# One-core attention and MLP kernel: the first head's roped halves written by the engines, its steps in a new order, and the last pair's tail reordered

## What is computed

```python
qc = layernorm(x @ W_cq)                      # 1024 x 192
q  = qc @ W_q        # 16 heads x (128 "nope" + 64 "pe")
kv = x @ W_ckv       # 16 heads x (64 "pe" + 128 "nope")
kn = layernorm(kv_nope);  k_nope, v = split(kn @ W_kv)
q_pe, k_pe = rope(q_pe), rope(k_pe)
attn_h = softmax(causal(q k^T / sqrt(192))) @ v
# side path: top-8 tokens of each of 8 gates, a small attention over them,
# its mean (one 128-vector for each gate) is added to two heads' output
x1 = layernorm(x + concat(attn_h + io) @ W_o)
up, gate = x1 @ ternary(W_up)^T, x1 @ ternary(W_gate)^T
out = layernorm(x1 + (silu(up) * gate) @ ternary(W_down)^T)
```

## Time and profile before

| what | us |
| --- | --- |
| three runs | 715.3, 719.58, 719.54; median 719.54 |
| profiled execution: its own time | 718.88 |
| profiled execution: span of the core | 717.1 |
| PE busy in the span | 657.5 (92%) |
| DVE, ACT, POOL busy | 468.7, 399.4, 366.4 |

### The profile page before, as it was taken

How to read it: one execution, slowest core, us unless ns; L and a number is a source line. 1 busy time by engine, 2 the same in 40 slices (tenths; PEclk the granted TensorE clock), 3 DMA queues, 4 the chain that set the end, 5 groups by cost and what they waited for, 6 DMA issues and landing times.

```text
span 717.1 us, 14209 instructions
## 1 busy us (share of the span) xinstructions
PE 657.5 (92%) x4502; PEld 594.9 (83%) x4502; DVE 468.7 (65%) x1294; ACT 399.4 (56%) x934; POOL 366.4 (51%) x327
## 2 busy tenths in 40 slices
...
GB/s 244 104 40 210 1 31 89 69 87 53 56 100 88 51 37 117 88 51 18 119 104 51 0 132 110 51 0 117 124 51 0 105 239 67 2 1 1 1 31 30
DMA packets 26895, 51.43 MB, mean 72 GB/s; under 512 B 3824, under 2 KB 17008, under 8 KB 26864
## 3 DMA queue, kind: packets, MB, share of 16 engines
...
...
## 4 chain that ended last, share of the span: by engine, by line
PE 57%; DVE 13%; ACT 10%; issue 10%; POOL 6%; SPq 2%; DMA 2%; DVEq 0%; ACTq 0%; POOLq 0%
PE J L804 9%; PE J L806 9%; PE J L805 9%; PE J L837 4%; DVE PTl L1252 3%; PE SC L824 3%; PE SC L827 3%; PE SC L828 3%; PE SC L826 3%; PE SC L825 3%; POOL rstd L706 3%; ACT kvraw L1207 3%; ACT Pb L1117 3%; ACT PTh L1100 2%; PE J L950 2%
## 5 line engine op out<-in xcount | busy, mean ns | idle before, releaser
L1252 DVE TENSOR_TENSOR PTl<-J,PTh 128x512 fp32r<-128x512 f32 (+1 forms) x192 | 102.2, 553 | 81.8 <-ACT PTh L1100 81.1
L1117 ACT ACTIVATE Pb<-SC,nm 128x128 f32<-128x128 f32 (+7 forms) x128 | 94.7, 740 | 52.2 <-DVE nm L1316 51.4
L1316 DVE CUSTOM_DVE_ANT_0 SC<-SC,mask 128x128 f32<-128x128 f32 (+7 forms) x128 | 97.3, 760 | 34.6 <-PE SC L828 31.2
L1100 ACT ACTIVATE PTh<-J 128x512 fp32r<-128x512 f32 (+1 forms) x192 | 88.1, 491 | 12.7 <-PE J L837 11.8
L804 PE MATMUL J<-PTh,Vh 128*128 128x256 f32 x320 | 88.5, 276 | 4.5 <-DVE PTl L1252 4.4
L837 PE MATMUL J<-ident,Pb 128*128 128x128 f32 x576 | 87.2, 279 | 4.7 <-ACT Pb L1117 4.4
L806 PE MATMUL J<-PTh,Vl 128*128 128x256 f32 x320 | 89.8, 280 | 0.0
L805 PE MATMUL J<-PTl,Vh 128*128 128x256 f32 x320 | 89.7, 280 | 0.0
L824 PE MATMUL SC<-KNh,QNh 128*128 128x128 f32 (+2 forms) x192 | 69.6, 363 | 8.1 <-DMA QS<-RQl 6.1
L837 PEld LDWEIGHTS J<-ident,Pb 128*128 128x128 f32 x576 | 64.2, 142 | 12.0 <-ACT Pb L1117 6.7
L804 PEld LDWEIGHTS J<-PTh,Vh 128*128 128x128 f32 x320 | 60.4, 189 | 9.8 <-DVE PTl L1252 6.7
...
## 6 DMA issues: line engine op xcount, KB each, us to landing
...
```

Of the source, the lines that this page charges most:

```text
L1100: return act.activation(o, i, ACT.Copy)
L1117: act.activation(Pb[i % 2][:, w], SC[i % 2][:, s], ACT.Exp, bias=nm[:, i % 2:i % 2 + 1], scale=-1.0, accum_out=sm[:, b, i:i + 1]).then_inc ...
L1252: dve.tensor_tensor(o, i, h.bitcast(F32), ALU.subtract).then_inc(done[kind], 1)
L1316: dve.tensor_tensor_reduce(out=SC[i % 2][:, s], in0=SC[i % 2][:, s], in1=mask[:, 128 * (7 - i):S], scale=-SCALE, scalar=HIGH, op0=ALU.add, ...
```

## The change

1. **First head's stacks by engines.** ACT and DVE write the two row halves of KD and KL straight from KX (`rk`: two copies and two subtractions of 64x512 in place of one each of 128x512), and DVE writes QS in `rope_q_first`. `stack_k_first` and `stack_q_first` with their twelve DMAs of 128 KB are gone. Head 1 still needs RKh, RKl, RQh and RQl: POOL writes them in new steps `rkrows` and `rqrows`.
2. **Prologue** in a new order: the qc tiles normalized in one operation each (192 columns in place of 128 and 64 twice), `qm` of odd tiles on 64 rows, W_qpe's and W_qps's high parts on ACT (POOL before), the first POOL product of `rkm` as a step `rks` of its own and earlier, `w0p` after the first `qc`, `kv` 1 before `qm`, `qm` 2 and 3 and `wb` last.
3. **Head 0** has a new list (FIRST_HEAD): `side` 0 and 1 in the slot of tile 1, `top8` split from `side` 1 and put in slot 3, `ab`, `qn` of head 1 earlier. SP loads the weights of pair 1 at the end of its prologue, and waits there for the top-8 and `rk_ready` before it loads the side path's weights and W_ip.
4. **Head 1:** `ropek` of pair 1 moves from the end of head 0 to slot 0 of head 1, behind `kvn`; `side` 10 to 12 one slot later; `io` from slot 6 to 4.
5. **All heads:** KD and KL become the two planes of one tile KK, RKh and RKl those of RK, so that `stk` is two DMAs of 512 KB in place of four of 256 KB.
6. **Last pair and MLP:** `wosp`, `rw` and the row additions later, `ln1`, `ln1n` and `ht` 0 one slot earlier, `ug` 0 and 1 in the last slot of head 15; the epilogue's start in a new order; LAG = 7; `res`, `ost`, `onorm` of the third quarter after the last `m`, and the last quarter done tile by tile (`last`, `lnorm`) with two stores.

The diff, cut to its core:

```diff
-LAG = 5
+LAG = 7
...
+        FIRST_HEAD = [
+            ("qk", 0, 0), ("exp", 0, 0), ("qmb", 0, 2), ("qmb", 0, 3),
+            ("qk", 0, 1), ("side", 0, 0), ("side", 0, 1), ("exp", 0, 1), ("kvs", 0, 3), ("kvag", 0, 1), *t(0, 0), ("rk", 0, 1),
+            ("qk", 0, 2), ("exp", 0, 2), ("qp", 0, 1), ("qps", 0, 1), ("ropeq", 0, 1), ("kvn2", 0, 1), *t(0, 1),
+            ("qk", 0, 3), ("qn", 0, 1), ("rqrows", 0, 1), ("kt", 0, 1), ("exp", 0, 3), ("rkrows", 0, 0), ("rkrows", 0, 1),
+            ("ab", 1, 0), ("pv", 0, 0), *t(0, 2), ("top8", 0, 0), ("kvn2", 0, 2), ("vsh", 0, 1), ("wkv", 1, 0),
+            ("qk", 0, 4), ("exp", 0, 4), ("side", 0, 2), *t(0, 3), ("stk", 1, 0), ("stq", 1, 0), ("kvn2", 0, 3), ("vs", 1, 0),
+            ("kt", 1, 0), ("side", 0, 3),
+            ("qk", 0, 5), ("pv", 0, 1), ("exp", 0, 5), ("kt", 1, 1), ("side", 0, 4), ("wosp", 2, 0), ("wqn", 2, 0), ("wqp", 1, 0),
+            *t(0, 4), ("qn", 1, 0), ("wo", 0, 0),
+            ("qk", 0, 6), ("side", 0, 5), ("exp", 0, 6), ("qn", 1, 1), *t(0, 5), ("wo", 0, 1), ("side", 0, 6), ("kv", 1, 0),
+            ("qk", 0, 7), ("kpe", 1, 0), ("side", 0, 7), ("exp", 0, 7), ("kv", 1, 1), ("pv", 0, 2), *t(0, 6),
+            ("side", 0, 8), ("kpe", 1, 1), ("kv", 1, 2), ("kv", 1, 3), ("side", 0, 9)]
...
-                    add(0, True, ("wtot", 0, 2), ("rowadd", 0, 0), ("rowadd", 0, 1))
-                    add(1, True, ("rowadd", 0, 2), ("rowadd", 0, 3), ("tern", 0, 8))
+                    add(0, True, ("wtot", 0, 2))
+                    add(1, True, ("rowadd", 0, 0), ("rowadd", 0, 1), ("rowadd", 0, 2), ("rowadd", 0, 3), ("tern", 0, 8))
                     add(2, True, ("tern", 0, 9))
                     add(3, True, ("tern", 0, 10))
                     add(4, True, ("tern", 0, 11))
-                    add(5, True, ("ln1", 0, 0))
-                    add(6, True, ("ln1n", 0, 0), ("ln1", 0, 1))
-                    add(7, True, ("ht", 0, 0), ("ln1n", 0, 1))
+
+            def late_steps():
+
+                add(4, True, ("ln1", 0, 0))
+                add(5, True, ("ln1n", 0, 0))
+                add(6, True, ("ht", 0, 0), ("ln1", 0, 1))
+                add(7, True, ("ug", 0, 0), ("ug", 0, 1), ("ln1n", 0, 1))
...
+                add(6, last, ("rw", 2, 0))
...
-                add(0, first, ("side", 0, 10))
-                add(1, first, ("side", 0, 11))
-                add(2, first, ("side", 0, 12))
+                add(1, first, ("side", 0, 10))
+                add(2, first, ("side", 0, 11))
+                add(3, first, ("side", 0, 12))
...
                 add(0, more, ("kvn", 1, 0))
+                add(0, first, ("ropek", 1, 0))
                 add(1, more and not first, ("qp", 1, 1), ("ropeq", 1, 0))
                 add(1, more, ("kvn2", 1, 0), ("stk", n, 0))
                 add(2, True, *t(h, 1), ("wo", m, 3))
...
+        PRO_PE = (each("qc", 0, 1, 2, 3) + each("kpe", 0) + each("qc", 4, 5, 6, 7) + each("kv", 0, 1) + each("qm", 0, 1) +
+                  each("ab", 0) + each("kpe", 1) + each("qp", 0) + each("qps", 0) + each("qn", 0) + each("kv", 2, 3) +
+                  each("kt", 0) + each("qm", 2, 3) + each("wb", 0))
+        PRO_ACT = (each("xs", 0, 1, 2, 3) + each("cs", 0) + each("w0", 0) + each("kpe", 0) + each("qnm", 0) + each("kv", 0, 1) +
+                   each("qm", 0, 1) + each("ab", 0) + each("qnm", 1) + each("kpe", 1) + each("rk", 0) + each("qn", 0) +
+                   each("kvn2", 0) + each("kv", 2) + each("kt", 0) + each("kv", 3) + each("qm", 2))
+        PRO_DVE = (each("xs", 0, 1, 2, 3) + each("qc", 0, 1, 2, 3) + each("w0p", 0) + each("w0", 0) + each("qnm", 0) +
+                   each("w0k", 0) + each("qc", 4, 5, 6, 7) + each("kvs", 0) + each("qms", 1) + each("qm", 0, 1) + each("kvs", 1) +
+                   each("kvnh", 0) + each("ab", 0) + each("ropeq", 0) + each("qn", 0) + each("rk", 0) + each("kvs", 2) +
+                   each("kt", 0) + each("qms", 3) + each("wb", 0))
+        PRO_POOL = (each("wkp", 0) + each("wkv", 0) + each("qrs", 0) + each("wqpl", 0) + each("rks", 0) + each("qrs", 1) +
+                    each("rkm", 0) + each("kvnh", 0) + each("rks", 1) + each("rkm", 1) + each("rqrows", 0) + each("vsh", 0) +
+                    each("kvnh", 1) + [("wqn", 1, 0), ("wosp", 1, 0)])
...
-            if q >= 1:
+            if q in (1, 2):
                 a += {1: [one("res", q - 1)], 2: [one("ost", q - 1)], 4: [one("onorm", q - 1)]}.get(e, [])
             return a
 
-        EPILOGUE = [one("ug", 0), one("ug", 1), *t(NH - 1, 7), ("wo", NH - 1, 2), one("ht", 1), ("pv", NH - 1, 3), one("m", 0),
-                    one("ln1", 2), one("ug", 2), one("ug", 3), one("m", 1), ("wo", NH - 1, 3), one("ln1n", 2), one("ug", 4),
-                    one("m", 2), one("ln1", 3), one("ug", 5), one("m", 3), one("dn", 0), one("ug", 6), one("ln1n", 3),
-                    one("m", 4), one("dn", 1)]
+        EPILOGUE = [("wo", NH - 1, 2), *t(NH - 1, 7), one("ug", 2), one("ht", 1), one("m", 0), one("ug", 3), ("pv", NH - 1, 3),
+                    one("m", 1), one("ln1", 2), one("ug", 4), one("m", 2), ("wo", NH - 1, 3), one("ln1n", 2), one("ug", 5),
+                    one("m", 3), one("ln1", 3), one("ug", 6), one("m", 4), one("ln1n", 3)]
         for n in range(7, NM):
             EPILOGUE += mlp_steps_of(n)
-        EPILOGUE += [one("m", NM - 2), one("onorm", 2), one("m", NM - 1)] + [one("dn", n) for n in range(NM - LAG, NM)]
-        EPILOGUE += [one("res", 3), one("ost", 3), one("onorm", 3)]
+        EPILOGUE += [one("m", NM - 2), one("dn", NM - 7), one("m", NM - 1), one("res", 2), one("ost", 2), one("onorm", 2)]
+        EPILOGUE += [one("dn", n) for n in range(NM - 6, NM)] + [one("last", 0), one("last", 1), one("lnorm", 0), one("lnorm", 1)]
...
-                        sp.dma_start(KD[b][rows, :].bitcast(F32), RKh[r, :].bitcast(F32)).then_inc(stacked[b], 16)
-                        sp.dma_start(KL[b][rows, :].bitcast(F32), RKl[r, :].bitcast(F32)).then_inc(stacked[b], 16)
+                        sp.dma_start(KK[b][rows, :, :].bitcast(F32), RK[r, :, :].bitcast(F32)).then_inc(stacked[b], 16)
...
-            stack_q_first(0)
-            stack_k_first(0)
-            stack_k_first(1)
-            stack_q_first(1)
+            load("wkv", 1)
+            load("wqp", 1)
+            sp.wait_ge(side_dve, 2)
+            sp.wait_ge(head1_lo, 1)
+            for n, src in enumerate((W_sq, W_sk, W_sv, W_io[:, 0:128])):
+                sp.dma_start(wside[:, n, :], src).then_inc(ld_ws, 16)
+            sp.wait_ge(rk_ready, 1)
             sp.dma_start(wip, W_ip.rearrange("(k p) n -> p k n", p=128)).then_inc(ld_wip, 16)
...
+            eng.tensor_copy(QS[0][0:64, q], x0[0:64, :]).then_inc(rq0_mul, 1)
             eng.wait_ge(rq0_mul, 2 * c + 2)
-            eng.tensor_tensor(RQl[:, q], X[:, 0, q], RQh[:, q].bitcast(F32), ALU.subtract).then_inc(rq0_ready, 1)
-            if c == 1:
-                eng.wait_ge(rq0_ready, 2)
-                eng.sem_inc(rq_ready, 1)
+            eng.tensor_tensor(QS[0][64:128, q], x0[0:64, :], QS[0][0:64, q].bitcast(F32), ALU.subtract).then_inc(rq0_ready, 1)
...
+                    if kind == "rks":
+                        q = half(c)
+                        gp.wait_ge(k0_swapped[c], 32)
+                        gp.wait_ge(ld_cs[c], 16)
+                        gp.tensor_tensor(KX[:, 1, q], KX[:, 1, q], sinT[:, q], ALU.mult).then_inc(rk0_mul[c], 1)
+                    if kind == "rkrows":
+                        q = half(c)
+                        gp.wait_ge(rk0_mul[c], 3)
+                        gp.tensor_copy(RKh[:, q], KX[:, 0, q]).then_inc(head1_hi, 1)
+                        gp.wait_ge(head1_hi, c + 3)
+                        gp.tensor_tensor(RKl[:, q], KX[:, 0, q], RKh[:, q].bitcast(F32), ALU.subtract).then_inc(head1_lo, 1)
+                        if c == 1:
+                            for n in range(2):
+                                gp.wait_ge(rk0_ready[n], 2)
+                            gp.wait_ge(head1_lo, 4)
+                            gp.sem_inc(rk_ready, 1)
+                    if kind == "rqrows":
+                        q, x0 = half(c), roped_q(c)[0]
+                        gp.wait_ge(rq0_mul, 2 * c + 1)
+                        gp.tensor_copy(RQh[:, q], x0).then_inc(head1_hi, 1)
+                        gp.wait_ge(head1_hi, c + 1)
+                        gp.tensor_tensor(RQl[:, q], x0, RQh[:, q].bitcast(F32), ALU.subtract).then_inc(head1_lo, 1)
+                        if c == 1:
+                            gp.wait_ge(rq0_ready, 2)
+                            gp.wait_ge(head1_lo, 2)
+                            gp.sem_inc(rq_ready, 1)
...
-                    pe.wait_ge(k0_stacked[c], 64)
-                    pe.wait_ge(q0_stacked[c], 32)
+                    pe.wait_ge(rk0_ready[c], 2)
+                    pe.wait_ge(rq0_ready, c + 1)
...
-                        copy(RKh[:, half(c)], KX[:, 0, half(c)]).then_inc(rk0_mul[c], 1)
```

(16 more changed lines are left out.)

186 lines of the change are left out of this document (83 added, 103 removed).

## The result

| | us |
| --- | --- |
| kernel before | median 718.41 of 4 runs (715.3 to 719.58) |
| changed kernel | median 707.86 of 4 runs (707.47 to 708.24) |
| ratio | 0.986, 95% interval 0.9825 to 0.9895 |
| changed kernel, profiled execution | 707.47; span 705.6 |

The change makes the kernel 1.4% faster, 10.6 us by the medians; the forecast was 708. The sum is near, its terms less so. This table takes the start of the first tile of scores of some heads as milestones, in the profiled execution of each kernel (718.88 and 707.47 us, so 11.4 us apart).

The account below looks back on a forecast made before the run. PE bounds the MID passes; elsewhere time goes to DVE's prologue and chains of waits. Head 0 and prologue -12, head 1 +6.8, MID 0, last pair -4.5, end -1.3 sum to -11.0: from 718.88 to 708 us, range 698 to 717.

Parts of the forecast that it names:

- prologue: Up to head 0's first tile: 3.3 us gained, the tile starting at 29.9 us instead of 33.29.
- port: Prologue and head 0: DVE operations using SBUF held up by POOL, 0.1 us for each of ten, 1.0 us in all.
- first tile to head 1: Head 0: 8.7 us gained, with the fifth tile at 44.8 us and head 1 beginning at 87.7 to 88.4.
- head 1: Head 1: 4.2 us lost, as the swap of QX queues behind a stack that waits for the later ropek.
- clock behind it: Start of head 2: PE at the lower clock after its wait, costing 2.6 us.
- loop, the other five pairs: The MID passes: no change, 0 us, with ends of -3 and +3.
- last pair and end: Last pair and MLP: 4.5 us gained in the last pair and 1.3 at the end.
- Rival C: Prologue and head 0: some 17 DVE operations each held 1.0 us by POOL, +15 us, 723 us; chance 0.08.
- top-8 chain: Head 0: from MAX8 to PE's side 2 takes 4.8 us, ending near 51 us.
- rival A: Head 1: the swap doesn't wait behind the stacks, so head 1 gains 3.5 us; 698 us, chance 0.20.
- PE's wait for `ht`: End of head 15: the 2.73 us wait goes, and 1.2 us of lower clock behind it.
- the sign that I had named: End of the kernel: in the trace after, a last dn about 5 us before the span's end.

Follow-up runs that it names:

- experiment 4: Changed kernel with POOL's second half of the first rope waiting for DVE's first KL rows: 706.7 us, ratio 0.9836.
- Experiment 7: Changed kernel with edits of experiment 1 and experiment 4, 15 useless PE matmuls, and POOL's V split waiting for the one-hot: 690.23 us, ratio 0.962.
- 5 to 7: Changed kernel with top-8, side 2 and 3 later: 709.62 us; with experiment 1's and experiment 4's edits: 696.25, plus 18 useless matmuls: 693.96; then Experiment 7.
- experiment 1: Changed kernel with head 2's K stack issued after the swap of QX on SP's queue: 697.0 us, ratio 0.9712.
- 3: Kernel before with only ropek of pair 1 moved to slot 0 of head 1, behind kvn: 725.29 us, ratio 1.0076.
- 9: Two kernels, each the changed kernel with one edit: K stack as four 256 KB DMAs, 708.07 us; LAG back to 5, 707.75 us.
- 8: Kernel before with all last-pair and MLP edits: 712.0 us, ratio 0.9889; with only the moves of weights and row additions: 718.17 us, ratio 0.9986.
- experiment 2: Changed kernel with ropek of pair 1 put back at the end of head 0: 703.69 us, ratio 0.9798.

## Why the prediction was right, and where it wasn't

| step | forecast | changed | what the runs say |
| --- | --- | --- | --- |
| prologue | -3.3 | -1.4 | port, mis-sized |
| first tile to head 1 | -8.7 | -6.7 | port shown by 4 and 7, clock fits 5 to 7; mis-sized |
| head 1 | +4.2 | +2.5 | mechanism shown by 1 and 3 |
| clock behind it | +2.6 | +1.4 | first pair 75.13 us for 73.75; mis-sized |
| loop, the other five pairs | 0 | +0.3 | 9: not the merged stacks |
| last pair and end | -5.8 | -7.6 | 8: -5.6 in its profiled execution, -7.1 by medians |
| sum | -11.0 | -11.5 | |

**Prologue.** What ends PE's waits was forecast rightly in the main; most of what follows is about sizes. The term that was mis-sized here is the port: I took 0.1 us for each of ten DVE operations, and three of them lost 2.3 us (experiment 4). With them free the first tile starts at 30.26; I had said 29.9. The mean of the earlier trace rows, by which I chose 0.1, was of two operations with next to no POOL work beside them; the one held row, i8f in the earlier trace rows, was the one to go by. Rival C had the size right, 0.7 to 1.0 us each, but not the number of operations on the path.

**Head 0.** -12 was forecast by head 1, -8.1 came. 2.0 us were lost by the first tile, and the fifth came at 47.12 for 44.8, 2.3 late. The top-8 chain was 4.5 us, as I said (4.8), but i8f and i8d in it and the one-hot behind it are held for some 2 us together, which I had copied from the old trace as their own durations. Tile 5 came at 58.85 for 55.5. There the clock was at 0.50 over 55 to 60, where I had allowed 0.6 us for it; tile 5 to tile 6 took 10.05 us, not 8.7. Experiment 7 takes both away and reaches head 1 at 85.33.

**Head 1.** The queue and the place of the wait are as forecast, and its length nearly: product 8.92 us behind the rope's end (9.3 forecast), QS landed 4.5 us after `ropeq` (4.6), PE stood 9.5 us (12). The term was 1.7 us too high: the norm came 0.4 earlier, each of two ropes took 10.9 us instead of 11.3, and the gap between them 8.9 instead of 9.3. PE without that wait would have reached head 2 some 7.0 us sooner than before, not 9.5, which is why it stood less; the sum doesn't use this. The clock behind it was costed at half of 5.3 us. The matmuls ran at 1.2 GHz for 5.9 us (137.9 to 143.8), but the pair was only 1.4 us longer than before and 1.9 longer than in experiment 1: the lower clock did not cost half of its time.

The moved step cost what it cost because of one `stk` that stood in front of a swap: rival A's time, 698, is what the kernel takes (697.0) when that order is turned. Rival A as a claim on the hardware is false, as the swap did wait, twice over: 5.7 us to be issued (by experiment 1), and then 7.7 us from issue to product, where experiment 2's swap, with no stack just ahead, took 3.4.

**Last pair and end.** Of the 5.8 us I gave 3.9 to PE's wait for `ht` and the clock behind it. That wait is gone (none over 1.5 us after 645, as forecast), but 2.4 us come from head 14, which I put at nothing: PE's wait for DVE to read out `rw` 2 went there (8). LAG, to which I gave part of the end's 1.3 us, does nothing measurable (9). PE's last matmul ends 7.2 us before the span's end, 6.3 in the kernel before; the sign that I had named, a last `dn` about 5 us before it, did not come.

That -11.0 met -11.5 is luck in its size, as errors stood against each other: head 0 and prologue promised 3.9 us too much, head 1 and its clock were charged 2.9 too much, the tail was 1.8 too low. The clock in head 15 alone, which no term foresaw, makes 2 us of difference between executions. In the chances, a tenth of the remaining 0.32 added to 0.68 makes 0.71 for "faster by over 1%", not 0.73.
